# VectorE scales half the tiles of a fourth unit before the seeds, its first root operation goes behind the picks, the last stage tile gets two homes, and one rank copy goes ahead of the seeds

## The reference, cut to what matters

```python
m_j = node_features @ W1[:D];  m_i = node_features @ W1[D:]
pre = m_j[:, None, :, :] + m_i[:, :, None, :] + b1            # per pair (i, j), 128 features
msg = gelu(layernorm(pre, g1, be1))
agg = einsum('bijo,bij->bio', msg, adjacency)                 # summed over j with the edge's weight
updated = layernorm(concat(node_features, agg) @ W2 + b2, g2, be2)
x = layernorm(x + updated)
```

## Time and profile before

| | before |
|---|---|
| median of 3 runs | 3537.92 us |
| the profiled execution's own time | 3535.7 us |
| its span | 3533.7 us |
| TensorE busy | 3198.2 us (91%) |
| ScalarE busy | 3042.6 us (86%) |
| VectorE busy | 3008.2 us (85%) |
| GpSimd busy | 2104.7 us (60%) |
| granted TensorE clock, mean | 0.973 |

### The profile page before, as it was taken

One profiled execution on the slowest core, in us unless ns is written; L12 is line 12 of the kernel. 1 busy time (PEld: TensorE's weight loads), 2 busy tenths in 40 slices (PEclk: granted clock), 3 DMA queues, 4 the chain that ended last, 5 costly groups with the idle time before them and its releaser, 6 DMA issues.

```text
span 3533.7 us, 87356 instructions
## 1 busy us (share of the span) xinstructions
PE 3198.2 (91%) x26504; PEld 2943.3 (83%) x26505; DVE 3008.2 (85%) x6816; ACT 3042.6 (86%) x8038; POOL 2104.7 (60%) x2628
## 2 busy tenths in 40 slices
PE   4899999999989998999998999989999999999988
PEld 2788888888878888888887888888888888888887
DVE  3689988889978898888898888988888988888987
ACT  3788889898968988888987989888889898989887
POOL 3556665556645566655566555666555666555652
PEclk7999999999989999999999999999999999999999
DMA  2333333233332333323332323333323333323231
GB/s 73 106 98 106 104 115 106 88 107 106 101 102 83 110 106 97 123 94 96 111 107 94 109 87 106 107 97 122 102 89 111 106 98 121 108 82 111 91 96 45
DMA packets 284214, 355.29 MB, mean 101 GB/s; under 512 B 28208, under 2 KB 242736, under 8 KB 283696
## 3 DMA queue, kind: packets, MB, share of 16 engines
q1 hardware_dynamic: 250928, 231.55, 22.5%
q0 software_dynamic: 32768, 117.47, 8.8%
HBM read 223.09 MB, written 125.83 MB: 99 GB/s over the span
## 4 chain that ended last, share of the span: by engine, by line
PE 50%; DVE 22%; issue 10%; ACT 10%; POOL 6%; DMA 1%; DVEq 1%; ACTq 0%; SPq 0%; POOLq 0%; PEldq 0%
PE agg_even_ps L1323 9%; PE z_even_ps L1364 8%; PE z_odd_ps L1364 8%; PE agg_odd_ps L1323 6%; DVE pick L1078 6%; DVE spread L1107 4%; POOL table L514 3%; DVE msg L1053 2%; PE z_even_ps L1360 2%; PE z_odd_ps L1360 2%; ACT tmp L713 2%; ACT root L658 2%; PE p_ps L1175 2%; PE p_ps L1244 2%; PE agg_odd_ps L1244 2%
## 5 line engine op out<-in xcount | busy, mean ns | idle before, releaser
L713 ACT ACTIVATE tmp<-nbr,r_sb 128x128 f32<-128x128 f32 x4032 | 1262.5, 389 | 24.9
L1078 DVE SCALAR_TENSOR_TENSOR pick<-rank,root_p 128x512 f32<-128x512 bf16 (+3 forms) x1536 | 914.8, 625 | 98.3 <-PE z_odd_ps L1364 53.2
L514 POOL DMA_INDIRECT table<-stage,row_id x512 | 747.0, 1459 | 155.8 <-issue 145.1
L1107 DVE SCALAR_TENSOR_TENSOR spread<-nbr 128x512 f32<-128x512 bf16 (+3 forms) x1536 | 814.8, 557 | 6.5 <-PE agg_even_ps L1323 5.5
L698 ACT ACTIVATE msg<-msg 128x768 f32<-128x768 f32 x768 | 646.7, 842 | 16.0 <-issue 8.3
L529 POOL COPY root_extra<-root_p 128x32 f32<-128x32 f32 (+4 forms) x768 | 315.7, 411 | 518.7 <-ACT root_p L672 514.7
L1364 PEld LDWEIGHTS z_odd_ps<-mi_g,pick 128*128 128x128 f32 x4608 | 587.1, 198 | 26.0 <-issue 0.5
L1323 PE MATMUL agg_odd_ps<-spread,msg 128*128 128x128 f32 x4608 | 597.5, 281 | 4.5 <-issue 3.6
L1364 PE MATMUL z_odd_ps<-mi_g,pick 128*128 128x129 f32 x4608 | 600.6, 282 | 0.0
L1364 PEld LDWEIGHTS z_even_ps<-mi_g,pick 128*128 128x128 f32 x4608 | 567.1, 192 | 25.6 <-issue 0.2
L1364 PE MATMUL z_even_ps<-mi_g,pick 128*128 128x129 f32 x4608 | 579.0, 275 | 0.0
(11 more groups left out here) (219 smaller groups left out, 4609.4 us busy)
## 6 DMA issues: line engine op xcount, KB each, us to landing
nbr<-table SPq DMA_DIRECT2D x128, 640.0 KB, 5.0
adj_g<-in_adj SPq DMA_DIRECT2D x32, 1024.0 KB, 5.9
nbr_root<-table SPq DMA_DIRECT2D x128, 256.0 KB, 5.4
nbr_extra<-table SPq DMA_DIRECT2D x384, 70.0 KB
nbr_extra<-table SPq DMA_DIRECT2D x128, 90.0 KB
nbr_extra<-table SPq DMA_DIRECT2D x256, 40.0 KB
x_g<-in_x SPq DMA_DIRECT2D x32, 256.0 KB, 3.1
table<-stage,row_id POOLq DMA_INDIRECT x512, 4.6
```

What stands on the lines that cost most here:

```text
L514: pool.indirect_dma_start(table[q], bass.IndirectOffsetOnAxis(ap=row_id[:, jt * TB + it:jt * TB + it + 1], axis=0), stage[:, jt, it, :], N ...
L713: last = act.activation(tmp[:, c % 2, n - FROM[u], :], half_row, ACT.Identity, scale=r_sb[:, c % 2, n - FROM[u]:n - FROM[u] + 1])
L1078: ins = dve.scalar_tensor_tensor(into.rearrange("p k n -> p (k n)"), rank[:, it % 2, span], float(MARK + t), root_p[:, it % 2, span], ALU. ...
L1107: ins = dve.scalar_tensor_tensor(into, ranks(nbr[:, it, jt:jt + count, A_RANK:A_ROOT]), float(MARK + t), nbr[:, it, jt:jt + count, A_ADJ:A ...
```

## The change

1. `HELPED` becomes (8, 9, 10, 11): VectorE scales 3 spots of unit 8 too.
2. ScalarE copies `rank` (L677, tile 2) ahead of that step's preparation in the step of `S_SEED`, so ahead of the seeds, and not behind them.
3. VectorE's first root operation (L939 for jt = 0) goes from slot 0 to slot 3 of step 10, behind the picks and the first spread.
4. The array `half` is gone. The intermediate values of the roots stand in the root places of the stage rows; ScalarE's first square waits for the scatters of the graph before.
5. Stage has two homes for its last block: `rows_sb` as before, and `last_rows`, used by every second graph. Waits for the scatters of block 3 thus ask for those of two graphs back (`written`).
6. `own` is put into `sqi` and waits for the matmul that read it, not for the roots.
7. GpSimd: the sorting goes ahead of the preparation in a step, and the fourth tile's extra columns come two steps later, at step 20: behind `x_y`, ahead of `pre_g` and `edge`.

```diff
-HELPED = (9, 10, 11)
+HELPED = (8, 9, 10, 11)
-T_RANK, T_ROOT, T_EXTRA = 3, 4, (6, 6, 5, 6)
+T_RANK, T_ROOT, T_EXTRA = 3, 4, (6, 6, 5, 8)
...
-        half = sb("half", [P, TB, N])
-        stage = sb("stage", [P, TB, TB, ROW])
+        rows_sb = sb("rows_sb", [P, TB, TB, ROW])
+        last_rows = sb("last_rows", [P, TB, ROW])
+        def stage(q, jt):
+            return last_rows[:, :, :] if jt == TB - 1 and q else rows_sb[:, jt, :, :]
+        def halfway(q, jt):
+            return stage(q, jt)[:, :, A_ROOT:ROW]
+        def written(jt, a):
+            return max(a - 1, 0) if jt == TB - 1 and isinstance(a, int) else a - 1 if jt == TB - 1 else a
...
-                    own = half[:, 0, :].rearrange("p (t o) -> p t o", t=TB)
+                    own = sqi[:, :].rearrange("p (t o) -> p t o", t=TB)
-                        wait_alone(pool, p_mask, a * TB)
+                        wait_alone(pool, p_fill, a * NF - (NF - F_MIT - 1))
...
# gpsimd, steps
-                if a is not None:
-                    prepare(a, (i + AHEAD) // GC % 2 ^ 1, s)
                 k, t = cx.sorted(i)
                 if k is not None:
                     sort(cx.tiles + k, k, t)
                 if a is not None:
+                    prepare(a, (i + AHEAD) // GC % 2 ^ 1, s)
                     scatter(a, (i + AHEAD) // GC % 2 ^ 1, s)
...
# scalar, prepare
-                        if not is_int(a, 1):
+                        if not is_int(a, 2 if jt == TB - 1 else 1):
                             for it in range(TB):
-                                act.wait_ge(p_scat[jt][it], a * 16)
-                        act.copy(stage[:, jt, :, A_ADJ:A_MJ], p.rearrange("p (i n) -> p i n", i=TB)).then_inc(p_ev, 1)
+                                act.wait_ge(p_scat[jt][it], written(jt, a) * 16)
+                        act.copy(stage(q, jt)[:, :, A_ADJ:A_MJ], p.rearrange("p (i n) -> p i n", i=TB)).then_inc(p_ev, 1)
...
-                        act.activation(half[:, jt, :], root[:, jt, :], ACT.Square).then_inc(p_sq, 1)
+                        if not is_int(a, 2 if jt == TB - 1 else 1):
+                            for it in range(TB):
+                                act.wait_ge(p_scat[jt][it], written(jt, a) * 16)
+                        act.activation(halfway(q, jt), blocks(root[:, jt, :]), ACT.Square).then_inc(p_sq, 1)
...
# scalar, steps
+                k, t = cx.sorted(i)
+                if k is not None and s == S_SEED:
+                    sort(cx.tiles + k, k, t)
                 if a is not None:
                     prepare(a, (i + AHEAD) // GC % 2 ^ 1, s)
-                k, t = cx.sorted(i)
-                if k is not None:
+                if k is not None and s != S_SEED:
                     sort(cx.tiles + k, k, t)
...
# vector, prepare
-                    if (s, slot) == (S_ROOT + jt, 0):
+                    if (s, slot) == (S_ROOT + jt, 3 if jt == 0 else 0):
                         dve.wait_ge(p_sq, a * TB + (jt + 1))
-                        dve.scalar_tensor_tensor(half[:, jt, :], v, EPS, half[:, jt, :], ALU.add, ALU.mult).then_inc(p_new, 1)
+                        dve.scalar_tensor_tensor(halfway(q, jt), blocks(v), EPS, halfway(q, jt), ALU.add, ALU.mult).then_inc(p_new, 1)
```

More of the change, by code:

```diff
@@ L265, in adj_resnorm_kernel, with blocks @@
         XL = len(LOADS) * 16
+        def stage(q, jt):
+            return last_rows[:, :, :] if jt == TB - 1 and q else rows_sb[:, jt, :, :]
+        def halfway(q, jt):
+            return stage(q, jt)[:, :, A_ROOT:ROW]
+        def blocks(row):
+            return row.rearrange("p (i n) -> p i n", i=TB)
+        def written(jt, a):
+            return max(a - 1, 0) if jt == TB - 1 and isinstance(a, int) else a - 1 if jt == TB - 1 else a
         def ranks(rows):
@@ L483, in prepare @@
                     for jt in range(TB):
-                        if not is_int(a, 1):
+                        if not is_int(a, 2 if jt == TB - 1 else 1):
                             for it in range(TB):
-                                wait_alone(pool, p_scat[jt][it], a * 16)
-                        last = pool.tensor_copy(stage[:, jt, :, A_MJ:A_RANK], mj_g[:, jt, :].unsqueeze(1).to_broadcast([P, TB, D]))
+                                wait_alone(pool, p_scat[jt][it], written(jt, a) * 16)
+                        last = pool.tensor_copy(stage(q, jt)[:, :, A_MJ:A_RANK], mj_g[:, jt, :].unsqueeze(1).to_broadcast([P, TB, D]))
                     last.then_inc(p_copy, 1)
@@ L604, in prepare @@
                         act.wait_ge(r_fill, a * TB + (jt + 1))
-                        act.copy(ranks(stage[:, jt, :, A_RANK:A_ROOT]), t_ps[:, 0, :].rearrange("p (i n) -> p i n", i=TB)).then_inc(r_ev, 1)
+                        act.copy(ranks(stage(q, jt)[:, :, A_RANK:A_ROOT]), t_ps[:, 0, :].rearrange("p (i n) -> p i n", i=TB)).then_inc(r_ev, 1)
                 if s == S_SUP:
@@ L662, in prepare @@
                             act.wait_ge(p_seed, a + 1)
-                        act.activation(half[:, jt, :], root[:, jt, :], ACT.Square).then_inc(p_sq, 1)
+                        if not is_int(a, 2 if jt == TB - 1 else 1):
+                            for it in range(TB):
+                                act.wait_ge(p_scat[jt][it], written(jt, a) * 16)
+                        act.activation(halfway(q, jt), blocks(root[:, jt, :]), ACT.Square).then_inc(p_sq, 1)
                     if s == S_ROOT + jt:
                         act.wait_ge(p_new, a * TB + (jt + 1))
-                        act.activation(half[:, jt, :], half[:, jt, :], ACT.Square, bias=cube_col[:, :], scale=CUBE_K).then_inc(p_cube, 1)
+                        act.activation(halfway(q, jt), halfway(q, jt), ACT.Square, bias=cube_col[:, :], scale=CUBE_K).then_inc(p_cube, 1)
             def sort(n, k, t):
@@ L1174, in prepare @@
                         for mt in range(TB):
-                            last = mm(dst, stage[:, mt, it, A_ADJ:A_MJ], sup[:, mt, :], start=(mt == 0), stop=(mt == TB - 1))
+                            last = mm(dst, stage(q, mt)[:, it, A_ADJ:A_MJ], sup[:, mt, :], start=(mt == 0), stop=(mt == TB - 1))
                     if s == S_PROD + 1:
```

6 lines of the change are left out of this document (2 added, 4 removed).

## The result

The changed kernel takes 3453.69 us (median of 4 runs, 3450.89 to 3456.15) against 3539.41 us for the kernel before in the same comparison (4 runs, 3535.61 to 3546.71): a ratio of 0.9755, 95% interval 0.9737 to 0.9773. I had forecast 3526.0 and a range from 3502 to 3550. The sign and the mechanism at the seeds were right; the size was not. 12 us were forecast and 86 came.

A forecast was written before the change was run, and what follows sets the result against it. Bound: the seeds' pace first, then VectorE's, from unit 9 to 12. Terms -18.6 + 10.3 - 3.6 = -11.9 us on the profiled 3535.7 gave 3523.8, plus 2.2 for the median: 3526, range 3502 to 3550.

The forecast's parts named there:

- Unit 8 helped: VectorE takes three of unit 8's scalings from ScalarE: cost 0, as VectorE's wait for the square covers it.
- Rank copy first: Rank copy ahead of the seeds on ScalarE: TensorE's 1.47 us wait only moves one product group later, worth 0 alone.
- Root operation behind the picks: At the seeds, VectorE works during its 4.16 us wait: gain 0.6 us a graph, 18.6 us in all.
- What is late next is VectorE itself: VectorE has no gap from L942 to msg of unit 10, so the 0.6 us gain is handed on undiminished.
- Clock: TensorE's low clock moves from unit 11 to unit 12 in 10 more graphs: +10 us.
- (b): Rival: the low clock falls on unit 12 in every graph, +9 us, 3547, slower; chance 15%.
- Two homes: Second home for block 3 removes ScalarE's scatter wait, paying in three graphs at units 20 to 21: -3.6 us.
- Extra columns and GpSimd's order: On GpSimd after the scatters, x_y comes directly, the columns follow, pre_g and edge stay where they were: 0.
- (a): Rival: the spreads behind the root operation escape GpSimd's additions, 1.1 to 1.2 us a graph, 3500; chance 17%.
- (c): Rival: GpSimd's gapless chain from root copy to own is late against earlier units, +0.6 us a graph, 3557; chance 8%.
- (d): Rival: the root operation on VectorE is blocked too, +0.3 us in 31 graphs and +10, 3555; chance 4%.
- (e): Rival: nothing comes out, the 0.6 us is given back in later steps or to the low clock, 3538; chance 18%.

The follow-up runs named there:

- the kernel with slot 0: The changed kernel with the first root operation back in slot 0, ahead of the picks, all else as changed: 3496.35 us, ratio 0.9874 to the kernel before.

## Why the prediction missed

**What bounds the kernel** was read rightly for the seeds: the root operation's wait and what is queued behind it. I stopped there. The same kind of row stood in step 20 of the trace before: two picks of 2.6 us or more in nine graphs, though not in the middle graph that I read. I did not look for it because the waits name no releaser for a blocked instruction: it counts as busy.

**Unit 8 helped**: 0 forecast, 0 found.

**Rank copy first**: "worth 0 alone" with everything on ScalarE 0.2 us later. The mechanism is as described (unit 10 comes 1.7 us earlier, and unit 11 then 1.9 us later behind it than without the copy's move), the price is the 0.24 us a graph that I left out of the sum.

**Root operation behind the picks**: this is the term of the seeds that was mis-sized, 0.6 us a graph against 1.58 less from unit 9 to 12 with the slot alone, and 1.35 with the rank copy's price in it. The two spreads were blocked, as I let them be, but for 1.56 us and not 2.7, and of this nothing was seen in the end: msg of unit 9 waits for ScalarE's `r_sb` at 1723.67, which stands behind Gelu and the table load. I had this case as the far bound (1.1 to 1.2 us, the next operation of VectorE waiting for ScalarE's second square) and took the nearer row. By its own experiments the slot is worth 34 us alone and 43 with the rest. The sign that I named, L939 waiting 90 us or less, came with the slot alone (76.8 us in that trace) and not with the whole change (125.3).

"What is late next is VectorE itself" holds: unit 12 waits 1.90 us for msg L1070. But 0.36 us are given back from unit 12 to 14. In the rows the root operation of the third block takes 0.95 us (1731.34) and not 0.68, beside a GpSimd instruction on the extra columns (0.91 us from 1730.84); in the kernel with slot 0, which meets no such instruction there, the give-back is missing (8.37 us). That is a reading of two traces and was not tested by itself.

**Clock**: +10.3 us stand in the sum (ten graphs at 1.0 us give 10.0) for a low clock at unit 12 in more graphs; it did not come. Unit 12 to 13 takes 5.9 us in four graphs of the changed kernel, three before. The mean granted clock rose from 0.973 to 0.983, and this middle graph has none at 1.2 GHz. Its window (length, busy PE, PEld, DVE, ACT, POOL, clock, DMA) shows a granted clock of 1.00:

```profile
1690.00:1793.00 103.00, 96.98 (x825) 89.58 (x824) 89.19 (x211) 93.44 (x249) 63.39 (x81) 1.00 0.34 107
```

against a clock of 0.50 in the earlier trace rows. TensorE's idle before unit 11 (1.7 us, for Gelu) and before unit 12 (1.9 us) were not followed by a fall. Three graphs were too few to carry a rule, and rival (b) fell with it.

**Two homes**: 3.6 us forecast, bounds 0 and 44. The waits for scatters fell by 37.7 us (44.4 to 6.7), but they fell to 18.8 us in 7 graphs already when only the root operation's slot was changed. What is left for the home is 14 us of direct waits at most; its own share of the time stays open. The three graphs behind the 3.6 us (unit 20 to 21 in 5.9 us) are gone, but with columns and home undone only one of the kind is left as well, so that does not tell either.

**Extra columns and GpSimd's order**: the step that failed. "x_y, which was 4 us behind them, now comes directly; the columns, 4 us, follow, and pre_g and edge stay where they were", and I priced it at 0. In the middle graph the places came out as said: `pre_g` starts 7.66 us behind the start of unit 19 before (1808.77 and 1801.11) and 7.99 after (1766.14 and 1758.15). I asked only when each product is needed, and found slack for all. What counted was which of VectorE's instructions each one holds up. In step 19, which the columns leave, VectorE takes 3.28 us from its first pick to msg before and 2.54 after, in the mean, and unit 20 waits for that msg: 0.69 us a graph of the table's 1.3 from 19 to 21. The other 0.61 is not even over the graphs of the trace before: eight have the slow pair, in four the wide addition falls on a spread of step 20 (2.8 us for one), three are those of the homes, and one long graph is 2.1 us longer than after. In the changed kernel the columns stand between `x_y` and the addition, which comes at least 7.48 us behind unit 19 in every graph but the last two, past the picks and spreads of step 20. Undoing it costs 2.15 us a graph.

**The rivals.** (a), 3500, had the seeds right for the wrong reason: the spreads did not escape, their block was hidden. (c) named the place but not the way: with the root slot alone units 19 to 21 do take 0.6 us more, because GpSimd comes nearer to the units (0.2 us behind unit 19 for 1.5) and not because it is late; the columns' move in the same change takes that away and more. (b), (d) and (e) did not come.

The Trainium skill, SBUF — State Buffer, section SBUF: two separate sides, makes the blocks at units 19 to 21 the same thing as those at the root operation: GpSimd and a VectorE operation with two inputs from SBUF exclude each other for the length of an instruction. The rows agree for the wide addition (two picks of 2.83 against 1.43 us). They do not for all of GpSimd's work: in the trace before, the 17 spreads of 512 columns that have only the narrow power operation `x_y` beside them (1.9 us long) take 0.68 us, as those with nothing beside them do, and the four that have only a wide addition (L472) beside them take 1.76.

## What to carry to other kernels

Where two engines block each other, list every instruction of the one, the short ones too, and see which instructions of the other it meets in each stage; a blocked instruction is booked as busy, so look for one shape with two durations, not for waits. Moving work in a queue changes where all behind it falls: price the collisions that go and come, not only the due times, and price them only where the held engine is the one that the next unit waits for. And when a bound has the stage's other engine as its reason, check that engine's timeline before taking the nearer row.

## What the runs showed of the hardware

The chips differ. The kernel before takes 3540 us on chip R and 3638 to 3662 on the others, where it was not traced. In the traces of the changed kernel's variants the waits for rows that come back from DRAM make the difference: with the columns undone, on chip 3 again, they come to 148.1 us at ScalarE's L727 and 69.9 at TensorE's L1287; the changed kernel on chip R has neither wait. Its graphs take 104.67 us in the mean and those 110.26; 3.1 us of the 5.6 stand between units 14 and 15, 1.7 between 18 and 19. A gain that depends on who is early can be there on one chip and hidden on the next.

GpSimd's instructions change their length by their place too. Its copy of 112 columns (L545) has a mean of 465 ns in the changed kernel and 582 with columns and home undone, its copy of 144 columns 435 and 322. That VectorE is what holds them up is likely, but was not tested.
